# Moving the spread of the head norms and the splitting of q and k into the MLP of the layer before the first down product (first layer of a four-layer transformer on one core)

## The reference, cut to what matters

```
def _L0_cond_ref(x, c, ...):
    h = modulate(rmsnorm(x, g1, D), scale_msa, shift_msa)
    qkv = h @ qkv_w.T + qkv_b
    q = rmsnorm(q, qg, HEAD_DIM)
    k = rmsnorm(k, kg, HEAD_DIM)
    q = q * HEAD_DIM ** (-0.5)
    attn = jax.nn.softmax(jnp.einsum('bhqd,bhkd->bhqk', q, k), axis=-1)
    o = jnp.einsum('bhqk,bhkd->bhqd', attn, v)
    x = x + gate_msa[:, None, :] * o
    h2 = modulate(rmsnorm(x, g2, D), scale_mlp, shift_mlp)
    m = jax.nn.gelu(h2 @ fc1_w.T + fc1_b, approximate=True) @ fc2_w.T + fc2_b
    x = x + gate_mlp[:, None, :] * m
```

## Time and profile before

| | us |
|---|---|
| median of 3 runs (1966.56 to 1967.98) | 1967.48 |
| the profiled execution | 1968.75 |
| its span in the trace | 1967.0 |
| PE busy | 1633.2 (83%) |
| DVE busy | 1260.5 (64%) |
| ACT busy | 934.4 (48%) |
| POOL busy | 382.4 (19%) |
| mean granted clock of PE | 0.869 |

### The profile page before, as it was taken

One profiled execution on the slowest core, in us unless ns is written; L12 is line 12 of the kernel. 1 busy time (PEld: TensorE's weight loads), 2 busy tenths in 40 slices (PEclk: granted clock), 3 DMA queues, 4 the chain that ended last, 5 costly groups with the idle time before them and its releaser, 6 DMA issues. The chain is left out here.

```text
span 1967.0 us, 37580 instructions
## 1 busy us (share of the span) xinstructions
PE 1633.2 (83%) x13794; PEld 1065.8 (54%) x13794; DVE 1260.5 (64%) x3174; ACT 934.4 (48%) x2095; POOL 382.4 (19%) x432
## 2 busy tenths in 40 slices
PE   7357977887799989999989898999788788878787
PEld 4124544455465556566666566666455556545565
DVE  5664676566666666666666667666776666676633
ACT  0224544544555555555555555555354434444345
POOL 1020111011111111111111111111332433243300
PEclk9957978887888898899898989898897888888869
DMA  6160332133143333333333334333387765766620
GB/s 172 48 151 13 88 92 63 31 92 80 50 116 82 83 97 85 93 93 93 91 95 89 93 87 99 85 97 87 74 104 89 86 53 103 89 95 46 101 9 25
DMA packets 198009, 163.22 MB, mean 83 GB/s; under 512 B 80108, under 2 KB 182004, under 8 KB 191684
## 3 DMA queue, kind: packets, MB, share of 16 engines
q1 hardware_dynamic: 189444, 153.14, 39.6%
q10 hardware_dynamic: 8384, 7.69, 1.4%
HBM read 98.05 MB, written 61.95 MB: 81 GB/s over the span
## 5 line engine op out<-in xcount | busy, mean ns | idle before, releaser
L1052 DVE TENSOR_REDUCE maxima<-score_bank 128x4 f32<-128x512 f32 x512 | 341.0, 687 | 170.2 <-PE score_bank L1338 169.4
L779 ACT ACTIVATE p_room<-st_bank 128x512 f32<-128x512 f32 x512 | 300.5, 597 | 204.5 <-PE st_bank L1363 135.9
L1363 PE MATMUL st_bank<-stack_room 64*128 64x128 bf16 x2048 | 244.9, 236 | 23.1 <-ACT p_room L779 15.2
L1421 PE MATMUL lin<-h2T,w_h 128*128 128x256 f32 (+1 forms) x640 | 227.9, 448 | 36.1 <-ACT h2T L667 32.5
L835 ACT ACTIVATE gelu<-lin 128x256 f32<-128x256 f32 (+1 forms) x320 | 119.0, 382 | 284.0 <-PE lin L1421 284.0
L1363 PEld LDWEIGHTS st_bank<-stack_room 64*128 64x128 bf16 x2048 | 149.4, 102 | 181.4 <-issue 132.4
L1338 PE MATMUL score_bank<-stack_room 62*128 62x128 bf16 x2048 | 211.6, 230 | 8.1 <-DVE maxima L1052 5.4
L563 POOL TENSOR_TENSOR part_low<-qk_rest,part_mid 96x512 bf16<-96x512 f32 x96 | 117.0, 1218 | 444.2 <-DVE part_mid L1038 444.2
L1447 PE MATMUL lin<-w_f,gelu 128*128 128x144 f32 (+1 forms) x1280 | 194.9, 301 | 0.0
L1338 PEld LDWEIGHTS score_bank<-stack_room 62*128 62x128 bf16 x2048 | 129.4, 100 | 99.1 <-issue 55.6
L549 POOL TENSOR_TENSOR rstd<-var,neg_half 128x2 f32<-128x2 f32 (+1 forms) x96 | 77.1, 803 | 543.2 <-DVE var L912 309.0
(11 more groups left out here) (194 smaller groups left out, 2819.5 us busy)
## 6 DMA issues: line engine op xcount, KB each, us to landing
stack_room<-stack_dram SPq DMA_DIRECT2D x96, 512.0 KB, 7.5
gates<-gates_dram SPq DMA_DIRECT2D x64, 288.0 KB, 4.3
stack_dram<-part_high SPq DMA_DIRECT2D x64, 288.0 KB, 3.3
norm_room<-stack_dram SPq DMA_DIRECT2D x32, 512.0 KB, 8.1
stack_dram<-part_mid SPq DMA_DIRECT2D x64, 192.0 KB, 2.6
stack_dram<-part_high SPq DMA_DIRECT2D x64, 144.0 KB, 3.2
stack_dram<-part_mid SPq DMA_DIRECT2D x64, 96.0 KB, 2.8
stack_dram<-part_low SPq DMA_DIRECT2D x64, 96.0 KB, 2.1
```

The source lines that it names most:

```text
L779: eng.activation(probs[:, i % PBUFS, :], st_bank[i % 2][:, :], ACT.Exp, scale=float(HD) ** -0.5)\
L1052: eng.tensor_reduce(maxima[:, b, CH * c:CH * c + CH], score_bank[i % 2][:, :].rearrange("p (h k) -> p h k", h=CH), AX_X, ALU.max)\
L1363: ins = eng.matmul(o, score_columns(1, g, b, c, j, HALF), score_columns(0, g, b, c, j, HALF), start=True, stop=flow_of(g) == "a")
L1421: return eng.matmul(lin[LIN_BANK[f"F{h}{T}"]][0:FCM[T], 0:GT // 2], w[:, cols], act[:, tok], **flags)
```

## The change

On PE, `spread_norms(L)` moves from in front of `values(J, 0)` to between `flip_rows(g, 1, 1)` and `down(g, 0)`, except in the first iteration (g = -1), where it stays. As J's scores 0 and 1 now stand ahead of it, T = 0 and 1 wait for their maxima, and scores 2 and 3 wait for `fit`. On DVE, `fit(L)` and the three `mid` move behind `last_parts(g, 1, 1)`, on ACT the three `high` behind `modulated(g, 1, 1)`. On POOL `rstd_of(g, 1, 1)` moves in front of `lows(L)`. SP's program is the same. It touches the iterations g = 0 to 5 (L = 2 to 7).

```diff
--- before.py
+++ after.py
@@ -591,11 +591,12 @@
                     rstd_of(M, 0)
                 if g >= 0:
                     rstd_of(g, 1, 0)
+                if g >= 0:
+                    rstd_of(g, 1, 1)
                 if L < NG and not layer_of(L):
 
                     lows(L)
                 if g >= 0:
-                    rstd_of(g, 1, 1)
                     add_mlp(g, 0)
                     add_mlp(g, 1)
 
@@ -812,15 +813,12 @@
                     copy_oT(g, 2)
                 if late:
                     values(J, 0)
-                if normed_heads:
-                    high(L, 0)
-                    high(L, 1)
                 if g >= 0:
                     copy_oT(g, 3)
-                if normed_heads:
-                    high(L, 2)
-                if g >= 0:
                     modulated(g, 1, 0)
+                else:
+                    for T in range(QKT):
+                        high(L, T)
                 if late:
                     values(J, 1)
                 if J < NG and not late:
@@ -836,6 +834,9 @@
                                        GELU[layer_of(g)]).then_inc(S["gelu_ready"], 1)
                     if h == 0:
                         modulated(g, 1, 1)
+                    if h == 0 and normed_heads:
+                        for T in range(QKT):
+                            high(L, T)
                 if g >= 0:
                     first_use("exp_table", g, ACT.Exp)
                 if J < NG:
@@ -1192,10 +1193,11 @@
                     normalise(g, 1, 0)
                 if normed_heads:
                     normalise(M, 0)
+                if g < 0:
                     fit(L)
                     for T in range(QKT):
                         mid(L, T)
-                if g >= 0:
+                else:
                     residual(g, 1, 0)
                     last_parts(g, 1, 0)
                     statistics(g, 1, 1)
@@ -1207,6 +1209,11 @@
                     maximum(J, 1)
                 if g >= 0:
                     last_parts(g, 1, 1)
+                if g >= 0 and normed_heads:
+                    fit(L)
+                    for T in range(QKT):
+                        mid(L, T)
+                if g >= 0:
                     residual(g, 0, 1)
                 if J < NG:
                     for i in range(2, AHEAD):
@@ -1302,6 +1309,9 @@
                 for T in range(QKT):
                     if T == 0:
                         need(eng, "qk_taken", L, 2)
+                    if T < 2 <= L:
+
+                        need(eng, "max_done", L - 1, T)
                     if T == 2:
                         need(eng, "qk_scaled", L, 0)
                     eng.matmul(score_bank[T % 2][0:QKM, :], spread[:, T * QKM:(T + 1) * QKM], norm_y[:, 1, :],
@@ -1326,12 +1336,18 @@
                 elif i == 0:
                     need(eng, "reordered", g, 1)
 
-                if i >= 2:
+                normed_heads = g + 1 < NG and layer_of(g + 1) == 0
+                if normed_heads and i // 2 == (1 if g else 0):
+
+                    need(eng, "qk_scaled", g + 1, (2, 1)[i % 2])
+                elif i >= 2:
                     need(eng, "max_done", g, i - 2)
+                elif normed_heads:
+
+                    need(eng, ("qk_taken", "norm_max")[i], g + 1, (2, 0)[i])
                 elif g + 1 < NG:
 
-                    name = "qk_taken" if layer_of(g + 1) else "qk_scaled"
-                    need(eng, name, g + 1, (2, 1)[i])
+                    need(eng, "qk_taken", g + 1, (2, 1)[i])
                 else:
                     need(eng, "max_done", g - 1, i - 2 + STEPS)
                 for j in range(CH):
@@ -1510,7 +1526,7 @@
                 if g >= 0:
                     flip_o(g, 2)
                     o_to_tokens(g, 3)
-                if L < NG and layer_of(L) == 0:
+                if g < 0:
                     spread_norms(L)
                 if late:
                     values(J, 0)
@@ -1536,6 +1552,8 @@
                 for T in up(g, 0):
                     some_scores(1 * (T in (1, 2)))
                 flip_rows(g, 1, 1)
+                if L < NG and layer_of(L) == 0:
+                    spread_norms(L)
                 down(g, 0)
                 some_scores(1)
                 down(g, 1)
```

## The result

The changed kernel takes 2011.63 us (median of 4 runs, 2005.54 to 2015.96) against 1967.02: a ratio of 1.0238, 95% interval 1.0211 to 1.0266. (The 1967.02 is the median of the three runs shown before and a fourth of 1961.41.) That is slower by 44.6 us; the forecast was 1999 us, 31.5 slower, in a range of 1979 to 2018. The sign was right and the time lies in the range.

What follows compares the result with a forecast made beforehand. No engine was taken as full (PE busy 83%), so order decides. Later attention starts (+24 us) and lost clock in attention (+7.5) made +31.5 on 1967.5, giving 1999 us, range 1979 to 2018.

Steps and rivals of the forecast that it cites:

- The entry: From `norm_y` into the MLP: without the spread ahead, the first remainder product comes 9.6 us earlier.
- The order on SP: SP's queue before attention: `load_max(J, 0)` waits behind the late stack load, so attention starts 4.4 us later in g = 2.
- on PE, ACT and DVE alone 2.4 us of the 9.6 are left: MLP up to the fifth score: the moved spread and `mid` use up all but 2.4 us of the gain.
- The clock in attention: Attention of J = 1 to 5: lower clock after PE's idle time costs 1.5 us each.
- +24 for the rest: From `norm_y` to the next first shifted score: 4.1 us longer, times six groups, 24 us.
- +7.5 for attention: Five attention stretches, first shifted score to `norm_y`: 1.5 us of lost clock each, 7.5 us.
- the wait for the DMA: Start of attention: PE waits for the DMA of `max_T`, some 6 us in each of six groups.
- the small transfer is not held up: SP's queue: `load_max` lands as soon as today despite the stack load; attention 2.4 us earlier per group, 1953 us; chance 8%.

Runs made afterwards that it cites:

- e2: The changed kernel with spread T = 2 behind `down(g, 0)` instead of ahead of it; 2005.2 us.
- e5: The changed kernel with stack loads L = 2 to 7 put off on SP behind the next iteration's `load_max(J, 2)` and `(J, 3)`; 2010.7 us.
- e6: e5 with spread T = 2 behind `down(g, 0)` as well; 1997.3 us.
- e1: The changed kernel with `load_max(J, 0)` and `(J, 1)` issued ahead of `load_stack(L)` in iterations 0 to 5; 2021.0 us.
- e4: The changed kernel with `load_max` ahead of `load_stack` and eight unread filler matmuls in PE's wait for `fit` T = 0; 2008.0 us.
- e11: e9 with spread T = 2 put back ahead of `down(g, 0)`, as the change has it; 2015.8 us.
- e9: e8 with `load_max(J, 0)` and `(J, 1)` ahead of `store_parts(L)` on SP; 1983.0 us, median of ten runs.
- e8: e7 with the load of stack 1 put off too, against the prologue's idle time of PE; 1981.3 us.
- e7: e6 with DVE's three `mid` moved behind `maximum(J, 8)`, `(J, 9)` and `(J, 10)`; 1991.0 us.

## Why the prediction was right, and where it wasn't

**The entry: right.** `modulated(g, 1, 0)` was forecast 6.5 us behind `norm_y` and is 6.5; the first remainder product 9.5, is 10.0; the wait for `fit` T = 0 1.5, is 1.65; the end of `mid` 23.7, is 25.2; the stack load 29.8, is 30.3; from the end of `mid` to the loads 6.1, is 5.1. The times run a little late because the half clock of the entry still holds in the first hidden products (two of them take 0.63 us at 342.69, 0.39 in the earlier trace rows), where I had the MLP at full clock. One reading was too narrow: the rests of the other five groups before are 37.8 to 38.3 us, up to 0.75 from g = 2's and not 0.4.

**The order on SP: real, but the second bound.** By this mechanism alone attention would have started at 375.3 in g = 2, 42.6 behind `norm_y` (forecast 42.0). It started 44.2 behind it. The 12.2 us from the loads' issue to the landing of `load_max` came out at 12.22, but on another path: `load_max` was issued 9 us behind the loads, since PE came late to the maxima, and took 3.2 to 3.5 us to land over the six groups, where it takes 2.5 in the kernel before. So the queue held it for a microsecond at most; in e2, where it is issued 7 to 8 us behind, it takes 4.5 to 5.2. e5 shows that taking the load away wins nothing, e2 against e6 suggests some 8 us once PE is faster. The Trainium skill (DMA: Bandwidth & Descriptors, "Queues, rings and completion order") allows a small DMA to finish ahead of a large one issued before it; here the small one landed at 375.22 and the last of the loads at 375.31, so in this case the lead was 0.09 us, and the rival by which `load_max` lands as soon as before is excluded.

**The step that failed: "on PE, ACT and DVE alone 2.4 us of the 9.6 are left".** It took the MLP's durations from rows at full clock and assumed that the clock would stay, with a wait of 1.5 us put in front of the first down product. The clock fell to 0.50 within 1.1 us of the end of that wait in all six groups, and the part from the first down product on took 24.7 us instead of 14.7. So PE's own path lost 6.6 us in g = 2 where I had it gain 2.4. I priced the waiting time and not what it does to the clock of all that follows. The rest of the step holds: in the groups with the change's order on PE and DVE that kept most of the clock, g = 1 of e5 and g = 4 of e1, attention starts 34.6 us behind `norm_y`, in g = 0 of e4 34.7, where the sum has 35.2. Of the 10 us that the second part grew by, the order takes 2.2 (14.7 to 16.9, both at 1.00, the second in e4) and the clock 7.8. The kernel before has a longer wait at the spread (2.41 us) and half clock too, but in front of the MLP, where the clock had fallen already, at the end of attention, and is back before the first down product; the change moves the wait to where PE has the most left to do. That it is the clock is shown by e4 and e5, where one kernel has both kinds of groups. That the wait brings the early fall is shown by the filler of e4 against e1 and by e11 against e9. It is not the whole rule: e5 has a group with the wait that kept most of the clock, and e9 two without it that lost it.

**The clock in attention: right in kind, low in size.** Forecast 1.5 us for each of five stretches, measured 2.6, 13 in all. I had put it down to idle time in front of attention, which is absent; in the change the clock in attention is 0.80 to 0.87, where the kernel before has 0.87 to 0.97. That this comes from an MLP that ends at half clock is not shown: e5 has two groups whose MLP ends at full clock, and the attention behind them takes 28.2 us in one and 31.6 in the other.

**The sum.** +24 for the rest measured 33, +7.5 for attention measured 13. `load_max` lands 1.2 to 1.8 us before attention starts in each group, so a forecast by the wrong bound came close. That was luck: of the signs that I named, the wait for the DMA is absent, and I had written that this would make the forecast wrong. For the total it didn't, for the mechanism it did.

Of the rivals, "the small transfer is not held up" would still have been slower: e5, in which it isn't (2.5 us to land), takes 2010.7 and not 1953.

What stays open: why attention stays at 32 us in e8 and e9, whose MLP runs at full clock (a wait of 3 to 8 us in front of attention is still there, but no run takes it away), and what decides, with the same order of work and the same waits just ahead, which groups of e5 and e9 keep the clock.

## What to carry to other kernels

A wait of PE is not priced by its length: ask at which clock the work behind it runs now and how much of it there is, and put unavoidable waits ahead of the stretch with the least PE work. When a step that ends in a queue of DMAs is delayed, list everything that stands behind it in that queue; and when two bounds come out within a few per cent of each other, removing either alone can show nothing, so test them together. The granted clock of each window belongs beside its length in every comparison.

## What the runs showed of the hardware

In g = 2 of the change the windows of two us have the granted clock at 1.00 from 346 to 350, at 0.95 from 350 to 352 and at 0.50 from 352 on, while PE was busy for 2.35 of the four us ahead of the fall, with one wait of 1.65 us among them. It stayed at 0.50 until 388, though PE was busy for nearly all of the MLP's second half. The Trainium skill (TensorE: Matmul & The Clock Gate, "The HAM clock gate") says that the clock follows how busy PE has been of late, and knows two states; the traces agree, at 0.50 and 1.00. No single long stop was needed for it here: the longest was 1.65 us. The same order of work with the same waits just ahead didn't always give the same clock (e5: 0.90 and 0.50 behind the wait of 1.65 us; e9: 0.99 and 0.59).

DVE's cast of `mid` takes 0.42 us where POOL is idle and 1.26 beside POOL's `lows` (0.89 where they overlap for less), before and after the move. In e7, e8, e9 and e11 no cast of the moved groups runs beside `lows`, and all of these take 0.42.
